# The down projection's weights prepared behind the first batch's gate and up products, and W13's norms taken by pairs of chunks

## What is computed

```python
# mixer: i, f, g = x@Wi.T, x@Wf.T, x@Wg.T
gate = sigmoid(f); v = silu(i) * (1 - gate)
o = scan over time of o = gate*o + v
o = o * rsqrt(mean(o*o) + EPS) * gnorm_w * g * sigmoid(g)
y = o @ Wo.T
x = x + layernorm(mixer(layernorm(x)))
# feed-forward
hidden = fwht(silu(z @ W1.T) * (z @ W3.T))   # 2048 wide
out = hidden @ W2.T
x = x + layernorm(ffn(layernorm(x)))
```

## Time and profile before

| what | value |
|---|---|
| median of 3 runs | 735.08 us (734.69 to 735.75) |
| profiled execution, its own time | 735.6 us |
| its span (first to last instruction) | 733.8 us |
| mean granted TensorE clock | 0.985 |
| PE busy | 702.8 us (96%) |
| DVE busy | 526.7 us (72%) |
| POOL busy | 308.6 us (42%) |
| ACT busy | 284.4 us (39%) |
| DMA | 105.73 MB, mean 144 GB/s |

### The profile page before, as it was taken

The page is one execution under the profiler, slowest core; times in us unless marked ns, Lnnn a source line. Parts: engine busy times, 40 slices in busy tenths (PEclk is TensorE's granted clock), DMA queues, the critical chain, the costliest instruction groups (busy, mean ns, idle before and its releaser), DMA issues.

```text
span 733.8 us, 11321 instructions
## 1 busy us (share of the span) xinstructions
PE 702.8 (96%) x4280; PEld 428.2 (58%) x4280; DVE 526.7 (72%) x877; ACT 284.4 (39%) x482; POOL 308.6 (42%) x268
## 2 busy tenths in 40 slices
PE   4899969999999999999999999999999999999996
PEld 2444434445444545457777677556666668876772
DVE  5997899895756838778847486786557856756564
ACT  5669736463542424433222232442322232313221
POOL 2947987453566845133451212232224530203112
PEclk9899979999999999999999999999999999999999
DMA  8952145364336474205353262261223341472102
GB/s 336 416 204 83 43 130 182 119 205 155 115 115 195 169 296 159 87 4 198 130 205 112 101 232 102 86 212 43 91 102 119 142 168 49 182 253 102 35 1 87
DMA packets 28199, 105.73 MB, mean 144 GB/s; under 512 B 2800, under 2 KB 7152, under 8 KB 23536
## 3 DMA queue, kind: packets, MB, share of 16 engines
q1 hardware_dynamic: 28144, 105.00, 40.4%
HBM read 81.92 MB, written 23.07 MB: 143 GB/s over the span
## 4 chain that ended last, share of the span: by engine, by line
PE 73%; DVE 13%; POOL 5%; DMA 4%; issue 2%; ACT 2%; DVEq 1%; SPq 0%; ACTq 0%; POOLq 0%
PE ps L577 24%; PE ps L578 23%; PE ps L579 23%; DVE ring L1224 2%; DVE ring L1086 2%; DMA ring<-W13t 2%; DMA ring<-L_attn_Wi 1%; DVEq L1048 1%; PE ps L629 1%; DVE ring L1230 1%; PE ps L719 1%; DVE st L1047 1%; POOL w2t L1392 1%; POOL hsp L1417 1%; DVE o_s L1140 1%
## 5 line engine op out<-in xcount | busy, mean ns | idle before, releaser
L577 PE MATMUL ps<-xb,ring 128*128 128x256 f16 (+1 forms) x704 | 227.1, 323 | 1.1 <-DVE ring L1245 1.1
L579 PE MATMUL ps<-xb,ring 128*128 128x256 f16 (+1 forms) x704 | 227.1, 323 | 0.0
L578 PE MATMUL ps<-xb,ring 128*128 128x256 f16 (+1 forms) x704 | 227.1, 323 | 0.0
L577 PEld LDWEIGHTS ps<-xb,ring 128*128 128x128 f16 x704 | 69.3, 98 | 47.3 <-issue 2.9
L578 PEld LDWEIGHTS ps<-xb,ring 128*128 128x128 f16 x704 | 69.0, 98 | 46.3 <-issue 1.8
L579 PEld LDWEIGHTS ps<-xb,ring 128*128 128x128 f16 x704 | 69.0, 98 | 42.8 <-issue 1.1
L1345 POOL TENSOR_TENSOR rstd<-var,neg_half 128x1 f32<-128x1 f32 x64 | 44.0, 690 | 110.1 <-DVE var L1323 42.3
L1417 POOL TENSOR_TENSOR hsp<-sga,hsp 128x512 f16<-128x512 f32 x34 | 42.7, 1265 | 112.8 <-ACT hsp L1005 112.8
L577 PE MATMUL ps<-ring 128*128 128x256 f16 x288 | 78.5, 273 | 0.0
L578 PE MATMUL ps<-ring 128*128 128x256 f16 x288 | 78.5, 273 | 0.0
L579 PE MATMUL ps<-ring 128*128 128x256 f16 x288 | 78.5, 273 | 0.0
(11 more groups left out here) (190 smaller groups left out, 1327.6 us busy)
## 6 DMA issues: line engine op xcount, KB each, us to landing
ring<-w_comb SPq DMA_DIRECT2D x24, 1792.0 KB, 7.3
ring<-W13t SPq DMA_DIRECT2D x16, 512.0 KB, 10.8
ring<-W13t SPq DMA_DIRECT2D x8, 1024.0 KB, 6.4
w_comb<-ring SPq DMA_DIRECT2D x8, 1024.0 KB, 8.5
rows<-L_attn_hidden_states SPq DMA_DIRECT2D x16, 256.0 KB, 5.1
w2t<-W2t SPq DMA_DIRECT2D x8, 512.0 KB, 12.5
res<-L_attn_hidden_states SPq DMA_DIRECT2D x16, 256.0 KB, 4.0
x_rows<-res SPq DMA_DIRECT2D x16, 256.0 KB, 3.8
```

The lines of the kernel that those rows point to most:

```text
L577: pe.matmul(dst, a_hi, b_hi, start=start, stop=False)
L578: pe.matmul(dst, a_hi, b_lo, start=False, stop=False)
L579: return pe.matmul(dst, a_lo, b_hi, start=False, stop=stop)
```

## The change

The loads of W2's units move behind W_o, the residual and half of W13. W2N, W2D, W2S, the butterflies and the H2 steps move to later places in the lists: before the Y steps come only W2's norms; H2.0 and H2.1 stand around ZT, H2.2 and H2.3 among the first gate and up products, H2.4 to H2.7 around UP.0.12. Butterfly temporaries are `gate`, `x1r`, `ot` (not `hsp` and `sga`). All D.0 steps move behind GA.0.14. The 14 hidden chunks of batch 0 from chunk 2 on lie in `ring` at 32 to 60 KB, where used-up W13 chunks lay, each once the W13 chunk there is stored; the raw pair, the sums and the slots of the combined weights move up to 60, 68 and 56/70/84 KB, and wait accordingly. XT.1 and F.1.0 stand in the first gate and up products, the rest of batch 1's projections behind H2.7. F.2 to G.2 now precede GP.1.0 on PE.

WN squares two chunks at a time (8 steps of two 1024-element instructions). WS makes both scales in one set of instructions of two elements; the bound becomes a step of its own, HB, behind WT.1.1 on DVE. In the lists of batches 2 and 3 a few steps change places, and PSUM banks are numbered anew.

The cut diff: of the lists only the stretches around the change are shown, unchanged code lines are left out but for the names of functions.

```diff
--- before
+++ after
@@ -31,157 +31,154 @@
-EARLY = 6
 PE_ORDER = """
-XT.0.0:4 XT.0.1:5 XT.0.2:6 XT.0.3:7 AN.0.0:0 AN.1.0:1 W2N.0.0:2 AN.2.0:3 W2N.1.0 W2N.2.0 F.0.0:4 W2N.3.0 W2N.4.0
-W2N.5.0 I.0.0:5 W2N.6.0 W2N.7.0 G.0.0:0 W2S.0.0:6 I.0.1:1 GC.0.0:7 F.0.1:3 G.0.1:4 AN.3.0:2 I.0.2:5 F.0.2:6
-G.0.2:7 I.0.3:0 F.0.3:3 G.0.3:1 H2.0.0:2 H2.0.1:4 H2.1.0:6 H2.1.1:5 H2.2.0:7 MS.0.0:0 Y.0.0:3 Y.0.1:1 Y.0.2:2
-Y.0.3:4 WS.0.0:6 H2.2.1:5 H2.3.0:0 H2.3.1:7 H2.4.0:3 H2.4.1:1 ZT.0.0:2 ZT.0.1:6 ZT.0.2:5 ZT.0.3:0 H2.5.0:4
-H2.5.1:7 GA.0.0:3 UP.0.0:1 H2.6.0:2 H2.6.1:6 GA.0.1:5 UP.0.1:0 H2.7.0:4 H2.7.1:7 GA.0.2:3 D.0.0 D.0.1 D.0.2
-UP.0.2:6 D.0.3 D.0.4 D.0.5 D.0.6 D.0.7 GA.0.3:5 D.0.8 D.0.9 D.0.10 D.0.11 UP.0.3:4 GA.0.4:7 UP.0.4:6 D.0.12
...
+XT.0.0:4 XT.0.1:5 XT.0.2:6 AN.0.0:7 XT.0.3:0 AN.1.0:1 GC.0.0:2 AN.2.0:3 F.0.0:4 I.0.0:5 G.0.0:7 I.0.1:6 F.0.1:1
+G.0.1:0 AN.3.0:3 I.0.2:4 F.0.2:5 G.0.2:2 I.0.3:7 F.0.3:1 G.0.3:6 W2N.0.0:3 W2N.1.0 W2N.2.0 W2N.3.0 W2N.4.0
+W2N.5.0 W2N.6.0 MS.0.0:0 W2N.7.0 W2S.0.0:4 Y.0.0:5 Y.0.1:2 WS.0.0:7 Y.0.2:1 Y.0.3:6 H2.0.0:0 H2.0.1:3 ZT.0.0:4
+ZT.0.1:7 ZT.0.2:5 ZT.0.3:2 H2.1.0:1 H2.1.1:6 GA.0.0:0 UP.0.0:3 GA.0.1:4 UP.0.1:7 GA.0.2:5 H2.2.0:2 H2.2.1:1
+UP.0.2:6 XT.1.0:0 XT.1.1:2 XT.1.2:3 XT.1.3:1 GA.0.3:4 H2.3.0:0 H2.3.1:2 UP.0.3:3 F.1.0:1 GA.0.4:7 UP.0.4:5
+GA.0.5:0 UP.0.5:6 GA.0.6:2 UP.0.6:4 GA.0.7:3 UP.0.7:7 GA.0.8:5 UP.0.8:0 GA.0.9:6 UP.0.9:2 GA.0.10:4 UP.0.10:3
+GA.0.11:7 UP.0.11:5 GA.0.12:0 H2.4.0:6 H2.4.1:2 UP.0.12:4 H2.5.0:3 H2.5.1:7 H2.6.0:5 H2.6.1:0 H2.7.0:6 H2.7.1:2
+I.1.0:4 G.1.0:3 I.1.1:1 F.1.1:7 G.1.1:5 I.1.2:0 F.1.2:6 G.1.2:2 I.1.3:4 F.1.3:3 G.1.3:1 GA.0.13:7 UP.0.13:5
+MS.1.0:0 GA.0.14:6 D.0.0 D.0.1 Y.1.0:4 Y.1.1:7 Y.1.2:5 Y.1.3:6 D.0.2 D.0.3 UP.0.14:4 D.0.4 D.0.5 D.0.6 D.0.7
+GA.0.15:7 D.0.8 D.0.9 D.0.10 D.0.11 UP.0.15:5 ZT.1.0:6 D.0.12 ZT.1.1:4 D.0.13 D.0.14 D.0.15 D.0.16 ZT.1.2:7
+D.0.17 ZT.1.3:5 D.0.18 D.0.19 D.0.20 D.0.21 D.0.22 ZT.1.4:6 ZT.1.5:4 D.0.23 ZT.1.6:7 D.0.24 D.0.25 D.0.26 D.0.27
...
 ACT_ORDER = """
...
+XT.0.0 AQ.0.0 XT.0.1 XT.0.2 AQ.1.0 XT.0.3 AQ.2.0 AT.0.0 AT.1.0 AT.1.1 AT.0.1 AT.1.2 AT.0.2 AT.2.0 AT.2.1 AT.2.2
+F.0.0 AT.1.3 AT.0.3 AT.2.3 I.0.0 AQ.3.0 G.0.0 WN.0.0 I.0.1 F.0.1 S.0.0 P.0.0 WN.1.0 G.0.1 WN.2.0 AT.3.0 AT.3.1
+P.0.1 I.0.2 AT.3.2 AT.3.3 F.0.2 S.0.1 G.0.2 WN.3.0 I.0.3 P.0.2 F.0.3 S.0.2 WN.4.0 G.0.3 S.0.3 WN.5.0 P.0.3
+WN.6.0 WN.7.0 WT.0.0 WT.0.1 YN.0.0 WT.1.0 YN.0.1 WT.1.1 H2.0.0 YN.0.2 H2.0.1 YN.0.3 ZT.0.0 ZT.0.1 ZT.0.2 ZT.0.3
+H2.1.0 H2.1.1 WT.2.0 WT.2.1 WT.3.0 WT.3.1 GA.0.0 GA.0.1 H2.2.0 H2.2.1 WT.4.0 UP.0.0 WT.4.1 XT.1.0 XT.1.1 XT.1.2
+XT.1.3 GA.0.2 H2.3.0 UP.0.1 H2.3.1 WT.5.0 UP.0.2 GA.0.3 WT.5.1 WT.6.0 WT.6.1 UP.0.3 GA.0.4 WT.7.0 WT.7.1 WT.8.0
...
 DVE_ORDER = """
...
+X1.0.0 X1.0.1 X1.0.2 X2.0.0 X1.0.3 X2.0.1 X2.0.2 X2.0.3 XT.0.0 XT.0.1 AN.0.0 XT.0.2 GC.0.0 AN.1.0 XT.0.3 AT.0.0
+AN.2.0 AT.1.0 AT.1.1 AT.2.0 AT.0.1 AT.2.1 AT.1.2 AT.0.2 AT.2.2 I.0.0 GD.0.0 GS.0.0 S.0.0 AT.1.3 G.0.0 AT.0.3
+P.0.0 AT.2.3 I.0.1 S.0.1 AN.3.0 G.0.1 P.0.1 HN.0.0 AT.3.0 AT.3.1 I.0.2 AT.3.2 AT.3.3 S.0.2 G.0.2 P.0.2 I.0.3
+S.0.3 G.0.3 P.0.3 MS.0.0 W2D.0.0 W2S.0.0 Y.0.0 WS.0.0 Y.0.1 YN.0.0 Y.0.2 YN.0.1 WT.0.0 Y.0.3 YN.0.2 Z1.0.0
+YN.0.3 Z1.0.1 H2.0.0 Z1.0.2 Z2.0.0 Z1.0.3 Z2.0.1 Z2.0.2 H2.0.1 Z2.0.3 ZT.0.0 ZT.0.1 ZT.0.2 ZT.0.3 WT.0.1 H2.1.0
+WT.1.0 H2.1.1 WT.1.1 HB.0.0 X1.1.0 X1.1.1 X1.1.2 X2.1.0 WT.2.0 X1.1.3 X2.1.1 X2.1.2 GA.0.0 X2.1.3 WT.2.1 H2.2.0
+UP.0.0 H2.2.1 GA.0.1 WT.3.0 XT.1.0 XT.1.1 XT.1.2 XT.1.3 UP.0.1 GA.0.2 WT.3.1 H2.3.0 UP.0.2 H2.3.1 WT.4.0 GA.0.3
+WT.4.1 UP.0.3 WT.5.0 WT.5.1 WT.6.0 GA.0.4 WT.6.1 UP.0.4 WT.7.0 WT.7.1 GA.0.5 WT.8.0 UP.0.5 WT.8.1 WT.9.0 WT.9.1
...
 POOL_ORDER = """
-S.0.0 X1.0.0 X1.0.1 X1.0.2 X1.0.3 FW.0.0 FW.0.1 FW.0.2 FW.0.3 FW.0.4 FW.0.5 FW.1.0 FW.1.1 FW.1.2 FW.1.3 FW.1.4
-FW.1.5 FW.2.0 FW.2.1 FW.2.2 FW.2.3 FW.2.4 FW.2.5 P.0.0 P.0.1 S.0.1 S.0.2 P.0.2 FW.3.0 FW.3.1 S.0.3 P.0.3 FW.3.2
-FW.3.3 FW.3.4 FW.3.5 FW.4.0 FW.4.1 Y.0.0 FW.4.2 FW.4.3 Y.0.1 Y.0.2 YN.0.0 FW.4.4 YN.0.1 Y.0.3 FW.4.5 YN.0.2
...
+S.0.0 X1.0.0 X1.0.1 X1.0.2 X1.0.3 P.0.0 FW.0.0 FW.0.1 P.0.1 S.0.1 P.0.2 S.0.2 FW.0.2 S.0.3 S.1.0 FW.0.3 P.0.3
+FW.0.4 FW.0.5 FW.1.0 Y.0.0 FW.1.1 FW.1.2 Y.0.1 YN.0.0 Y.0.2 YN.0.1 Y.0.3 YN.0.2 Z1.0.0 YN.0.3 Z1.0.1 Z1.0.2
+FW.1.3 Z1.0.3 FW.1.4 FW.1.5 FW.2.0 FW.2.1 FW.2.2 FW.2.3 FW.2.4 FW.2.5 X1.1.0 X1.1.1 X1.1.2 FW.3.0 X1.1.3 FW.3.1
+FW.3.2 FW.3.3 FW.3.4 UP.0.0 FW.3.5 FW.4.0 FW.4.1 FW.4.2 FW.4.3 UP.0.1 FW.4.4 UP.0.2 FW.4.5 FW.5.0 UP.0.3 FW.5.1
+FW.5.2 FW.5.3 UP.0.4 FW.5.4 FW.5.5 UP.0.5 FW.6.0 FW.6.1 UP.0.6 FW.6.2 FW.6.3 UP.0.7 FW.6.4 FW.6.5 FW.7.0 UP.0.8
+SA.0.0 UP.0.9 FW.7.1 FW.7.2 UP.0.10 FW.7.3 FW.7.4 UP.0.11 SA.1.0 FW.7.5 UP.0.12 SA.2.0 P.1.0 S.1.1 P.1.1 SA.3.0
...
 SP_ORDER = """
...
+ST.0.0 ST.0.1 ST.0.2 ST.0.3 RL.1.0 XL.1.0 RL.1.1 RL.1.2 XL.1.1 XL.1.2 RL.1.3 XL.1.3 AS.0.0 AS.1.0 AS.2.0 AS.3.0
+AS.4.0 AS.5.0 SL.0.0 AS.6.0 AS.7.0 SL.1.0 SS.0.0 SL.2.0 SS.1.0 LR.0.0 LR.0.1 SL.3.0 SS.2.0 SL.4.0 SS.3.0 ST.1.0
+ST.1.1 SL.5.0 SS.4.0 ST.1.2 ST.1.3 WL.1.0 SL.6.0 SS.5.0 XL.2.0 XL.2.1 XL.2.2 XL.2.3 SL.7.0 SS.6.0 LR.0.2 O.0.0
...
-        wn2 = sb("wn2", [P, 2, HC])
-        w_exp = sb("w_exp", [P, 2, HC])
+        wn2 = sb("wn2", [P, 2, HC // 2])
+        w_exp = sb("w_exp", [P, 2, HC // 2])
...
         def unit_tmp(m):
-            flat = {"hsp": hsp[:].rearrange("p a s t -> p (a s t)").bitcast(F32), "sga": sga[:].rearrange("p s t -> p (s t)"),
+            flat = {"gate": gate[:].rearrange("p s t -> p (s t)"),
-        UNIT_TMP = ("x1r", "hsp", "sga", "x1r", "hsp", "ot0", "ot1", "x1r")
+        UNIT_TMP = ("x1r", "gate", "x1r", "ot0", "ot1", "gate", "x1r", "ot0")
         def unit_before(m):
...
         def kb(at, size):
-        comb_raw = kb(32, 8).bitcast(F32).rearrange("p (c w k n) -> p c w k n", c=2, w=2, k=KC)
+        comb_raw = kb(60, 8).bitcast(F32).rearrange("p (c w k n) -> p c w k n", c=2, w=2, k=KC)
         def comb_sum(j):
-            return kb(40 + 8 * (j % 2), 8).rearrange("p (w s c m) -> p w s c m", w=2, s=2, c=2)
+            return kb(68 + 8 * (j % 2), 8).rearrange("p (w s c m) -> p w s c m", w=2, s=2, c=2)
         def quad(c, h):
...
         def slot_of(b, j):
+        def slot(b, j):
+            return kb((84, 70, 56)[slot_of(b, j)], 14)
         def comb_w(b, j, w, block, part):
-            at = kb(56 + 14 * slot_of(b, j), 14)
+            at = slot(b, j)
...
         def chunk(c):
-        def early(b, c):
-            return b == 0 and 2 <= c < EARLY
         def late(b, c):
         def hid(b, c, part):
-            if early(b, c):
-                return xb[:, 1, part, c - 2]
+            if b == 0 and c >= 2:
+                return kb(32 + 2 * (c - 2) + part, 1)
...
             def load_raw_pair(j, _):
-                    sp.wait_ge(up_mm, 2)
-                    sp.wait_ge(st_a[0], 32)
+                    sp.wait_ge(up_mm, 9)
+                    sp.wait_ge(st_a[0], 96)
+                    sp.wait_ge(st_a[1], 64)
...
             def store_sums(j, _):
-                sp.dma_start(w_comb[j, :, 3072:7168], kb(40 + 8 * (j % 2), 8)).then_inc(st_s[j % 2], 16)
+                sp.dma_start(w_comb[j, :, 3072:7168], kb(68 + 8 * (j % 2), 8)).then_inc(st_s[j % 2], 16)
             def load_combined(b, j):
...
-                    sp.wait_ge(up_mm, (10, 13, 16)[n])
+                    sp.wait_ge(up_mm, HC)
+                    if n > 0:
+                        for i in range(2):
+                            sp.wait_ge(st_s[i], 16 * (HC // 4))
+                        sp.wait_ge(d_mm, HC)
-                sp.dma_start(kb(56 + 14 * slot_of(b, j), 14), w_comb[j]).then_inc(ld_wc[n % SLOTS], 16)
+                sp.dma_start(slot(b, j), w_comb[j]).then_inc(ld_wc[n % SLOTS], 16)
...
-            for m in range(4):
-                load_unit(m)
-            sp.dma_start(had[:], hadamard).then_inc(ld_had, 16)
-            for m in range(4, UNITS):
-                load_unit(m)
-            for c in range(HC):
+            sp.dma_start(had[:], hadamard).then_inc(ld_had, 16)
+            for c in range(HC // 2):
+            for m in range(4):
+                load_unit(m)
+            for c in range(HC // 2, HC):
+                load_pair(c)
+            for m in range(4, UNITS):
+                load_unit(m)
...
             def ws(b, t):
-                pe.wait_ge(squared, max(squares_to["WN", c, 0] for c in range(HC)))
-                pe.matmul(bank("WS", b, t)[:, 0:2 * HC], ones[:], wn2[:].rearrange("p w c -> p (w c)"),
+                pe.wait_ge(squared, max(squares_to["WN", j, 0] for j in range(HC // 2)))
+                pe.matmul(bank("WS", b, t)[:, 0:HC], ones[:], wn2[:].rearrange("p w c -> p (w c)"),
             def w2_products(m, _):
...
             def xt(b, t):
-                if b == 1 and t == 0:
-                    act.wait_ge(d_mm, EARLY)
...
+                if n == KC:
+                    act.wait_ge(h2_mm, 12)
...
-                    act.wait_ge(h2_mm, 14)
+                    act.wait_ge(h2_mm, 16)
...
-                            act.wait_ge(st_s[0], 16 * HC // 4)
+                            act.wait_ge(d_mm, HC)
...
```

(73 more changed lines are left out.)

212 lines of the change are left out of this document (91 added, 121 removed).

## The result

The changed kernel takes **731.05 us** (median of 6 runs, 728.83 to 733.03), before 735.02 beside it: ratio 0.9945, 95% interval 0.9928 to 0.9963. So it is faster by 4 us, where 6.4 were forecast, and 731.05 lies inside the forecast's own range. Its times spread over 4.2 us, those of before over 1.1.

The account below looks back on a forecast made before the run. TensorE, busy 702.8 of 733.8 us, was the bound, so only idle time and slow clock could be won. 5.5 us by GA.0.2, 6.5 with D.0.0's wait; against the median 735.08 - 6.4 = 728.7 us, 8-in-10 range 722.5 to 735.0.

Parts of the forecast that it names:

- Part 1: Butterflies moved out of the projections: attention-weight splits at 0.66 us, P.0.0 at 33 instead of 46.71, Y.0.0 13 us sooner.
- Y.0.0 at 58.2: Start of the first Y step: P.0.3 at 54, then a pair of norms on ScalarE between; before 71.22.
- About 1.2 us idle is left ahead of Y.0.0: TensorE's remaining pause before Y, behind W2N and MS, once the 3.3 us wait for W2's diagonal is gone.
- From Y to the last transposition 13 us: Stretch from Y's end (68.8) to Z's last transposition (81.8): 21.0 us before, 12.4 by the walk, 13 taken.
- GA.0.0 at 86: Start of the first gate product, after H2.1 with 0.9 us for slow clock; 7 us won against 93.2.
- A wait of 1.9 us at GA.0.2: TensorE arrives at 96.4, but VectorE's 15.2 us of work before WT.2.0 ends at 98.3.
- Part 2: Norms by pairs save ScalarE 3 to 5 us and hide; the bound HB leaves the chain from Y to Z.
- Part 4: VectorE's work from Z's last split to WT.2.0: 15.2 us, ending at 98.3, bounds 94.3 to 101.5; 5.5 us won.
- C: Rival, more gain: splits miss butterflies, no GA.0.2 wait, no half clock at H2.1, later 1.1 us gone: 723; chance 0.13.
- B: Rival: VectorE becomes the bound, splits and butterflies excluding each other fully at 1.94 a pair: 732 to 735; chance 0.14.
- A: Rival, slower: GpSimd late for H2.7 if the second raw-pair load issues after about 170 us: 739; chance 0.13.
- D: Rival: the new order is as long, P.0.0 being bound by loads of W_i and W_g: 735; chance 0.03.

Follow-up runs that it names:

- e1: The changed kernel with 8 useless GpSimd adds beside VectorE's attention-weight splits: 738.69 us, ratio 1.0052 to before.
- e5: The changed kernel with unread products only in TensorE's pause at Z (24 behind H2.0.1, 3 behind ZT.0.0): 730.76 us, ratio 0.9940.
- e7: The changed kernel reordered only, with norms, butterflies and W2's diagonal moved behind P.0.3 and WS behind Y.0.2: 728.63 us, ratio 0.9916.
- e4: The changed kernel with unread products only in the pause ahead of Y.0.0 (6 behind W2N.6, 4 behind W2N.7): 728.87 us, ratio 0.9932.
- e9: e7 with unread products in Z's pause (28 behind H2.0.1, 3 behind ZT.0.0): 728.25 us, ratio 0.9909.
- e6: The changed kernel with unread products in both pauses, those of e4 and e5 together: 727.89 us, ratio 0.9908.
- e11: The kernel before the change with only W13's norms taken by pairs of chunks: 734.31 us, ratio 0.9994.
- e2: The changed kernel with W13's norms by single chunk again, four 512-element squares per WN step: 734.06 us, ratio 0.9981.
- e12: e9 with Y.0.2's power put ahead of YN.0.0's addition on GpSimd: 727.53 us, ratio 0.9900.
- e10: e7 with the chain from Y to ZT put first on ScalarE, GpSimd and VectorE, plus unread TensorE products (8 and 6): 734.22 us, ratio 0.9990.

## Why the prediction was right, and where not

**Direction and mechanism: right.** Part 1 came as walked: F.0.0 at 20.5, splits at 0.67, P.0.0 at 33.0 (33), P.0.3 at 54.4 (54), projections to 51.7 (51.2) without a pause. e1 shows the splits' part of it: 5.3 of the 13.7 us at P.0.0, at a worth of 7.6 us in the time.

**The terms that were off**, in the order of the path:

- *Y.0.0 at 58.2; it was 59.8.* "ACT does a pair of norms between" was right, but two more stood behind: GpSimd's FW.0.2 took 2.2 us ahead of S.0.3, whose sum MS needs (1.54 us of wait), and W2N.7 with W2's diagonal stood behind MS (0.87). About 0.6 of the 1.6 us is the clock, by e5 (59.17). e7, which only reorders these, starts Y at 57.15.
- *"About 1.2 us idle is left ahead of Y.0.0", costed at nothing else.* The largest miss. PE was idle 2.4 us in two pieces, and Y.0.0's products ran at 1.2 GHz until 64.2: Y ended at 72.5 for 59.8 + 10.6, 2.1 us late. The 1.2 GHz level was weighed at F.0.0 and H2.1, not here. e4 gives it back: 2.2 between medians.
- *From Y to the last transposition 13 us; 13.9.* It began 8.9 us behind Y's end, and the half clock was in the sum only for H2.1. The clock is 0.3 to 0.4 us by the medians of e5 and e9, 1.0 by e6 less e4, and 0.9 to 1.2 by where GA.0.0 starts in the traces of e5 and e9; so it can be all of the miss.
- *GA.0.0 at 86; 90.83.* The three together, and 0.2 on H2.1.
- *A wait of 1.9 us at GA.0.2; none.* DVE needed 12.7 us from its last Z split (87.66) to the end of WT.2.0 (100.36), not 15.2: the W13 splits took 1.62, 1.48, 1.09 and 0.75 us, and 1.65 had been charged for each of the four; HB took 2.2 for 3.4; 0.8 of waiting for ACT was not in the sum. PE came 4.8 us late, so it met them ready. In e6, where PE is at GA.0.2 at 97.01, WT.2.0 ends at 96.84 and there is still no wait, by 0.2 us.

Together 4.8 late less 1.9 saved: 2.9 of the 6.5 us are missing at GA.0.2, and 1.1 came back behind it, more than the 1.0 booked, as MS.1.0's new wait of 1.16 replaced four of 2.7 in all. e4, with its clock up at Y, has 728.87, and after's own fastest run 728.83. That this is the forecast is partly luck: about 1.0 us of Y.0.0's lateness and 0.9 of Z stand there against the 1.9 of the wait that did not come.

- **Part 2, "hides"**: wrong in after's order. Costed at nothing alone, which e11 confirms; but its cover, ACT's free time, was used up by Part 1, and e2 prices the pairs at 2 to 3 us. The forecast had them in the sum without naming it, since it took a chunk's period of 7.0 as it was.
- **Two slips of the sums.** The upper bound in Part 4 is 98.3 + 3.0 = 101.3, not 101.5. The forecast, C and half of B add up to 0.77, not 0.80, so the chances given for within and slower are a little low together.

**Rivals.** A (late for H2.7): the second raw pair was issued 17.6 us behind the first, 16 had been forecast and 28 feared, and PE meets no wait there:

```profile
148.85 0.38 SPq L527 DMA_DIRECT2D ring<-W13t  x1
...
166.44 0.37 SPq L527 DMA_DIRECT2D ring<-W13t  x1
```

B (DVE the bound, exclusion in full): the waits on the W13 split never came, and a pair costs 1.46 in e1. C (more): two of its parts, no wait at GA.0.2 and the later 1.1 us gone, happened; the others, a clock up at H2.1 and splits that miss the butterflies, did not. D: P.0.0 moved by 13.7 us.

## What to carry to other kernels

A move that takes work out of a pause can cost the clock in the next one, so walk the whole new order for pauses, and price each behind which wide products follow at twice their length; but check first that PE is what ends the chain behind it (behind after's Y it was, behind before's Z not, and filling was worth 2.2 us and nothing). An edit that is free alone is not free after another edit has eaten its cover: price it again in the new order. And before putting a chain first on several in-order engines, count its round trips between them: what stands between its steps may be what fills them, and steps released together may run into each other.

## What was not expected of the hardware

The clock's fall is not the same in every run of one program: the same 2.4 us of idleness ahead of Y ended in 0.50 in after's trace and in 1.00 in e5's, and four of the kernels that keep PE busy there spread over 0.8 to 1.3 us (e6, e7, e9, e12) instead of 4.2. Two kernels speak against a simple account: e4 spreads over 6.4 (1.3 without its longest, whose clock fell at F.0.0 and at MS.1.0), and e1, which leaves the pause, over 0.6. And operations of one column a partition on DVE take 0.16 us alone and up to 0.96 when they start within a GpSimd add (e10's rows above); others beside an add kept their 0.15 to 0.21 us. So a chain of small steps suffers from a busy GpSimd more than its length suggests.
